# Moving the first expert group ahead of the means in six unrolled rows

## What is computed

```
x = x + involution7x7(layernorm_c(x))      # conv1 -> bn -> relu -> conv2 gives 4 x 49 weights per pixel
t = tokens(x)
t = t + moe(layernorm_t(t))                # 16 experts, all run: silu(x w1) * (x w2), times w3, top-2 gate
x = image(t)
x = x + lowrank_conv3x3(layernorm_c(x))    # composed to one 3x3 convolution
t = tokens(x)
t = t + lstm(layernorm_t(t))               # along T = 56*56 = 3136 steps, batch 4
```

## Time and profile before

| | us |
|---|---|
| median of 3 runs | 3993.85 (3993.41 to 3995.58) |
| profiled execution, in all | 3996.03 |
| its span, first to last instruction | 3994.3 |
| TensorE busy (matmul) | 3584.6 |
| VectorE busy | 3374.4 |
| ScalarE busy | 2527.2 |
| GpSimd busy | 2156.5 |
| the six head rows | about 20 to 193 |

### The profile page before, as it was taken

How to read it: one execution, slowest core, us unless ns; L and a number is a source line. 1 busy time by engine, 2 the same in 40 slices (tenths; PEclk the granted TensorE clock), 3 DMA queues, 4 the chain that set the end, 5 groups by cost and what they waited for, 6 DMA issues and landing times.

```text
span 3994.3 us, 130407 instructions
## 1 busy us (share of the span) xinstructions
PE 3584.6 (90%) x35548; PEld 2659.6 (67%) x35548; DVE 3374.4 (84%) x21816; ACT 2527.2 (63%) x11668; POOL 2156.5 (54%) x3179
## 2 busy tenths in 40 slices
PE   6899999989899999999999999999989899988888
PEld 5666666666666666666666666666666666666665
DVE  6688888888888888888888888888888888888887
ACT  4366666666666666666666666666666666666565
POOL 6655565656565656555555555565655565652222
PEclk7955555555555555555555555555555555555555
DMA  5000000000000000000000000000000000000000
GB/s 74 2 1 1 1 1 1 1 1 1 1 1 1 1 1 1 1 1 1 1 1 1 1 1 1 1 1 1 1 1 1 1 1 1 1 2 1 1 1 1
DMA packets 44538, 11.06 MB, mean 3 GB/s; under 512 B 39914, under 2 KB 44011, under 8 KB 44491
## 3 DMA queue, kind: packets, MB, share of 16 engines
q1 hardware_dynamic: 42378, 10.05, 1.6%
q10 hardware_dynamic: 2112, 0.46, 0.1%
HBM read 7.29 MB, written 3.21 MB: 3 GB/s over the span
## 4 chain that ended last, share of the span: by engine, by line
PE 66%; DVE 14%; ACT 13%; issue 5%; POOL 1%; DMA 0%; DVEq 0%; ACTq 0%; POOLq 0%
PE GATES L1343 14%; PE YB L1163 10%; PE GATES L1413 9%; ACT O L747 7%; PE H1B L1157 7%; ACT G L743 6%; DVE O L998 6%; PE YB L1314 6%; PE TAPB L1150 6%; PE DB L1282 5%; DVE HR L1002 5%; PE DB L1144 3%; PE H2B L1190 1%; PE H1B L1190 1%; PE H2B L1138 1%
## 5 line engine op out<-in xcount | busy, mean ns | idle before, releaser
L743 ACT ACTIVATE G<-GATES 128x12 f32<-128x12 f32 x3136 | 571.1, 182 | 1206.8 <-PE GATES L1413 1195.2
L1413 PEld LDWEIGHTS GATES<-HR,VW 128*128 128x128 f16 x6272 | 421.4, 107 | 601.5 <-issue 556.7
L1343 PE MATMUL GATES<-HR,VW 128*128 128x4 f16 x3136 | 531.8, 170 | 306.9 <-DVE HR L1002 214.0
L989 DVE TENSOR_TENSOR_SCAN CT<-G,CT 128x12 f32<-128x12 f32 x3136 | 586.5, 187 | 247.8 <-ACT G L743 218.7
L747 ACT ACTIVATE O<-G 128x8 f32<-128x8 f32 x3136 | 663.2, 211 | 98.7 <-ACT G L743 0.2
L998 DVE RECIPROCAL O<-O 128x4 f32<-128x4 f32 x3136 | 568.3, 181 | 175.1 <-ACT O L747 0.3
L1409 PEld LDWEIGHTS <-VW 128*128 128x128 f16 x3136 | 457.3, 146 | 354.3 <-issue 317.7
L976 DVE SCALAR_TENSOR_TENSOR CT<-HIST,CT 128x4 f32<-128x4 f32 x3136 | 522.0, 166 | 126.9 <-DVE HIST L1008 13.1
L1413 PE MATMUL GATES<-H,VB 128*128 128x4 f16 x6272 | 619.3, 169 | 0.0
L1413 PE MATMUL GATES<-HR,VW 128*128 128x4 f16 x6272 | 614.5, 168 | 0.0
L1163 PE MATMUL YB<-HD,W 128*64 128x112 f32 x3840 | 596.0, 412 | 1.7 <-DVE HD L869 1.7
(11 more groups left out here) (245 smaller groups left out, 6993.2 us busy)
## 6 DMA issues: line engine op xcount, KB each, us to landing
out_dram<-OUT SPq DMA_DIRECT2D x112, 28.0 KB, 1.9
X<-in_x_dram SPq DMA_DIRECT2D x4, 672.0 KB, 10.9
STG<-in_L_ffn_w_dram SPq DMA_DIRECT2D x4, 512.0 KB, 12.7
U<-in_L_conv_U2s_dram SPq DMA_DIRECT2D x1, 972.0 KB
W<-in_L_ffn_w_dram SPq DMA_DIRECT2D x1, 512.0 KB, 12.0
X<-in_x_dram ACTq DMA_DIRECT2D x4, 112.0 KB, 3.2
S<-in_L_conv_S1s_dram SPq DMA_DIRECT2D x1, 108.0 KB
S<-in_L_conv_S2s_dram SPq DMA_DIRECT2D x1, 108.0 KB
```

The lines of the kernel that those rows point to most:

```text
L743: act.activation(G6[:, :, 2:5], gates[c][:, w, :, :], ACT.Tanh, scale=1 / GSCALE).then_inc(step_in, 1)
L989: dve.tensor_tensor_scan(CELL.rearrange("z b k -> z (b k)"), G6[:, :, :].rearrange("z b k -> z (b k)")[:, 0::2], ADD3.rearrange("z b k -> ...
L1343: return pe.add_instruction(mybir.InstMatmult(name=nc.get_next_instruction_name(), engine=mybir.EngineType.PE, start_tensor_calc=False, st ...
L1413: last = pe.matmul(gates[c][:, w, :, SLOT[g]], wt[:, g].rearrange("z m c -> z (m c)"), digit, start=False, stop=True, skip_group_check=True)
```

## The change

The table of the head rows puts the first group of experts (DB, VV and HD of group 0) and the first kernel row's first four taps and their product (TAPD, PROD) ahead of both means, differences and squares (MEAN, XC, SQ). Two waits are added in head rows: ACC's product waits for slot1_done, since the sum of the row before reads ACC, and H1 of group 0 waits for xs_done. The tables of the loops stay.

```
-        MEAN=(2, 6), MEAN_ORDER=(1, 0), XC=(4, 7), SQ=8, VAR=(15, 15), VE=16, RSB=(27, 27), RSC=28,
+        MEAN=(9, 11), MEAN_ORDER=(1, 0), XC=(10, 12), SQ=13, VAR=(15, 15), VE=16, RSB=(27, 27), RSC=28,
...
-        DB=s, VV=[(t + 1, t + 1) for t in s], DBS=[], HD=[t + 3 for t in s],
+        DB=[8] + s[1:], VV=[(9, 9)] + [(t + 1, t + 1) for t in s[1:]], DBS=[], HD=[11] + [t + 3 for t in s[1:]],
...
-        TAPA=[5] + [t + 4 for t in s[:NT - 1]], PA=[6] + s[1:NT], TAPD=[(t + 1, t + 1) for t in s[:NT]],
-        PROD=[(t + 2, t + 2) for t in s[:NT]],
+        TAPA=[5] + [t + 4 for t in s[:NT - 1]], PA=[6] + s[1:NT], TAPD=[(8, 8)] + [(t + 1, t + 1) for t in s[1:NT]],
+        PROD=[(9, 9)] + [(t + 2, t + 2) for t in s[1:NT]],
...
                         dve.wait_ge(tapd_done, 1 + 2 * NT * j + 2 * k + (h + 1 if lstm else 2))
+                        if k == 0 and h == 0 and not lstm:
+
+                            dve.wait_ge(slot1_done, 1 + j)
...
                 if k == 0 and lstm:
                     pe.wait_ge(xc_done, 1 + 2 * j + 2)
+                if k == 0 and not lstm:
+                    pe.wait_ge(xs_done, 1 + j)
                 expert_in(pe, H1B, 0, k).then_inc(h1_done, 1)
```

## The result

The changed kernel takes 4006.17 us (median of 9 runs, 4003.84 to 4007.41) where the kernel before takes 3995.07 us beside it: 11.1 us slower, ratio 1.0029 with a 95% interval of 1.0020 to 1.0038. The forecast was 8.1 us slower, 4002.0 us; the time lies in its range of 3996.5 to 4007.5. The profiled run was the shortest of the nine: 4003.84 us, span 4002.1 us.

The account below looks back on a forecast made before the run. The prediction took the loops' serial steps as 3800 us and expected only six head rows to change, each set by when its variance starts. 7.9 + 0.2 = 8.1 us on 3993.85 gave 4002.0 us, range 3996.5 to 4007.5.

Parts of the forecast that it names:

- the summed chain: Main case: six head rows' later variance delays group 1's PA, 8.1 us slower with waits; chance 0.62, range 3999.5 to 4004.5.
- the lost clock: Rival: TensorE's new idle time ahead of the variance costs its fast clock, 3.3 us more, 4005.3 us; chance 0.15.
- the sum: Slides of the six head rows added: 1.5 + 1.0 + 1.8 + 0.8 + 1.1 + 1.7 = 7.9 us.
- The chain: Head rows with experts: VV, ACC, XC 1, HD, XC 0, SQ, then variance, 3.10 us after VV starts.
- Rows 0, 1, 2 and 4: Head rows forecast longer by 1.5, 1.0, 1.8 and 1.1 us through a later variance.
- Row 3: Head row at 1.2 GHz: variance 1.03 us late, less 0.24 us of PA's slack, so 0.8 us longer.
- PA's 0.24 us of slack: Rows 3 and 4: group 1's taps end 0.24 us early for PA, taken off each row's slide.
- The clock rival: TensorE loses its fast clock from variance to group 1's PA in rows 0, 2, 5: 3.3 us; chance 0.15.
- the two waits: Added waits for slot1_done and xs_done in head rows: neither seen waiting, 0.2 us in all.
- the later VE: Behind group 1's additions on GpSimd: power RS_Y slides as far as VE, so costs nothing more.
- GpSimd's earlier first addition: Head rows: ACC comes 0.3 to 2 us earlier, but the gain is hidden behind the later PA of group 1.
- The rival that GpSimd's first addition counts: Head rows: PA of group 1 follows XC 0, 6 us faster, 3987.9; chance 0.08 shared with nothing seen.

Follow-up runs that it names:

- xc_first: Changed kernel with both XC of VectorE again ahead of VV, ACC and HD, TensorE's order as changed; 3999.47 us, 4.5 above the kernel before.
- hd_back: Changed kernel with HD of group 0 at t = 13, behind both XC; 4002.67 us, 7.4 above the kernel before.
- before_again: The kernel before, unchanged, run again for a second trace; 3991.51 us against 3991.39.
- before_waits: The kernel before with only the two added waits, in its own order; 3994.90 us against 3995.30 (ratio 1.0000).
- d0_only: The kernel before with the first D taps and ACC earlier, but behind the means and both XC; 3991.98 us against 3991.39.
- after_var18: Changed kernel with the six rows' variance at t = 18, behind group 1's taps; 3997.88 us, 2.9 above the kernel before.
- acc_back: Changed kernel with D taps D0 and product ACC back at t = 13 and 14, behind both XC; 3998.81 us, 3.5 above the kernel before.
- again: The changed kernel, unchanged, run again for a second trace; 4007.66 us, 12.6 above the kernel before.
- filler: Changed kernel with 12 unused matmuls ahead of the variance in all six head rows; 4005.00 us, 9.7 above the kernel before.

## Why the prediction was right, point by point

**How right, and how much of it was luck.** Direction and mechanism are those forecast. The time is 4.2 us above the forecast 4002.0: 1.2 us because the kernel before took 3995.07 us beside it and not 3993.85, 3.0 because the change cost 11.1 us and not 8.1. It lies in the wide range, but outside the 3999.5 to 4004.5 that I gave the summed chain alone, and nearest the 4005.3 of the lost clock. That the profiled span came at 4002.1 us, with 4002.4 forecast, is luck: that run was the shortest of nine, and row 3's cost was hidden by its clock. The 8.3 us of the six rows, where the sum had 7.9, match for the same reason: row 0 came 0.7 and row 5 0.6 us above the sum, row 3 0.9 below it. The chances had a slip too: "half of it to each side" of 0.62 is 0.31, not the 0.36 and 0.26 used.

**The chain is the one named.** VV, ACC, XC 1, HD and XC 0 run back to back, then SQ, then the variance. Counted from the row's start, row 5's variance was forecast at 5.54 us and came at 5.57 (5.58 in the second trace); row 0's at 5.92 at half clock and came at 5.69; row 2's at 6.89 and came at 6.81. xc_first shows that VectorE's order is over half of it; hd_back's PA in rows 3 and 5, 0.5 us earlier for HD's 0.53, that an instruction ahead of XC 0 is paid in full where the means are over before.

**Rows 0, 1, 2 and 4.** Forecast 1.5, 1.0, 1.8, 1.1 us; the first pair of traces has 2.2, 0.9, 1.8, 1.3. Row 0's excess is the full clock of before's variance there (0.95 us, 1.65 in the changed kernel): against before_again, at half clock too, it is 1.5. Against the same second trace rows 2 and 4 would be 0.9 and 0.8 only.

**Row 3 was mis-sized.** Its 0.8 us came out of a front at half clock, from which I took PA's 0.24 us of slack. With full clock in both kernels the row goes from 29.96 to 31.82 (1.9 us), with half clock in both from 31.96 to 34.20 (2.2 us). The first pair shows -0.1 only because one was traced at each clock. In the half-clock pair the variance is 0.8 us later (1.0 in the sum), PA 1.4 (0.8 in the sum, the variance itself now taking 1.21 us instead of 0.86), the power 2.2: behind the variance TensorE fell back to half clock.

**The clock rival came true in part**, at another place and size than put. It was given 3.3 us in rows 0, 2 and 5, for a slower stretch from the variance to PA; what happened is that in row 5 (and in row 3) the matmuls behind the variance went to half clock and the D taps of group 1 came late: 0.4 to 0.5 us in row 5, up to 0.8 in row 3. Row 5's 1.7 us became 2.3 this way (2.1 in the second trace), with its PA later by the 1.7 forecast. Row 0's slow variance isn't shown to be the gap's: the kernel before had it in its second trace too. Row 2 kept full clock.

**What was costed at nothing was nothing**: the two waits (before_waits), the later VE, GpSimd's earlier first addition, and the part of the row behind the power, which neither gave back nor added. I gave 0.2 us for the waits; 0 fits as well.

**The rival that GpSimd's first addition counts fell** with d0_only. The opposite test, after_var18, taught more: with the taps freed from the variance the changed order was still 2.9 us behind before, and its rows show DB waiting for SI behind SQ on ScalarE. The forecast listed what queues behind XC on VectorE and behind SQ's reader on TensorE; it left out what queues behind SQ itself on ScalarE. In the changed kernel that stall lay under TensorE's (row 5's SI ends at 179.07, DB of group 1 starts at 180.24), so it cost the forecast nothing.

**What stays open**: the rows of the second trace account for 10.5 of the 12.6 us measured beside it, those of the first for 8.3 of 11.1, and the first was the kernel's shortest run. Between traces with like clocks in rows 0 and 3 the rows give 8 to 10 us. The remaining 1 to 4 us, like the extra gains of xc_first, hd_back and acc_back, are about of the size by which two traces of one program differ in rows 2 and 3. Which order wins isn't in doubt.

## What to carry to other kernels

The largest wait in a profile needn't be worth anything: before moving work ahead of it, follow what the waiting engine needs next, and name the last thing in front of that. When a chain across engines (here means, XC, SQ, variance) has independent work queued behind each of its members, work put ahead of it on one engine delays that work on all of them; put such work where the chain leaves the engine idle, or put the chain's last, blocking member behind the work that others wait for (variance at t = 18: rows 1 and 5 shorter by 1.1 and 0.5 us here, 2.6 us in the median, which by itself is within the noise). And a front written by hand should be compared over two traces of each kernel before a term of a microsecond is believed.

## What the runs showed of the hardware

TensorE's clock in the same row of the same program differs between runs: row 3's front at 1.2 GHz in one trace of before and at 2.4 in another, 2 us of row length. Gaps of 1.1 to 1.7 us ahead of row 5's variance were followed by half clock in all four traces that had them (changed, again, hd_back, filler), and not when 24 small matmuls filled 1.34 us of it; gaps as long in rows 2 and 4 weren't, and after_var18 lost the clock in row 5 behind shorter waits. The granted clock as recorded isn't a safe witness at this scale: it reads 1.00 in the changed kernel where row 1's variance takes 1.66 us, and 0.50 in the kernel before where the same eight matmuls take 1.65 (columns as in the earlier trace rows; changed, then before):

```profile
55.80:57.50 1.70, 1.70 (x12) 1.70 (x12) 0.00 (x0) 0.01 (x1) 0.00 (x0) 1.00 1.34 175
```

```profile
52.60:54.40 1.80, 1.80 (x13) 1.73 (x12) 0.00 (x0) 0.04 (x1) 0.46 (x1) 0.50 1.38 158
```

For short stretches the duration of a known shape (0.95 or 1.65 us) tells the clock better. The Trainium skill (TensorE: Matmul & The Clock Gate, section "HAM oscillation — how this bites in real kernels") describes an array that goes back to half rate in the waits between bursts of matmuls. The waits that it describes are for transfers and longer than any of these gaps, so it neither foretells row 5's 0.97 and 0.56 us nor says why rows 2 and 4 were spared.
